# Two-layer decoder on one core: twelve conv pairs of the state-space stage beside the first mixture stage instead of eight

## The reference, cut to what matters

```python
x = x + attention(layernorm(x), Wq, bq, ...)            # A: 16 heads, causal
x = x + token_experts(layernorm(x), tokens, ctx)        # B: 4 experts, the context rows are the weights
x = x + mixture(layernorm(x), gate, w1, w2, shared)     # C: 8 experts, top 2, and one shared expert
x = x + state_space(layernorm(x), in_proj, conv, ...)   # D: the stage that the change is about
x = x + attention(layernorm(x), ctx, ctx)               # E: keys and values are the context rows
x = x + mixture(layernorm(x), ...)                      # F

def state_space(u):                                     # D
    xBC, z, A_log = split(u @ in_proj.T, [1536, 512, 64])
    xBC = silu(causal_conv(xBC, 4 taps, per channel) + bias)
    X, B, C = split(xBC, [512, 512, 512])               # 64 heads x 8;  8 groups x 64;  8 groups x 64
    dt = softplus(A_log)
    y = chunked_scan(X, -dt, B, C, chunk=128) + D * X / dt
    return (y * silu(z + z_bias)) @ out_proj.T
```

## Time and profile before

| | |
|---|---|
| median of 3 runs | 832.39 us |
| profiled execution | 829.35 us, its span 827.5 us |
| mean granted TensorE clock | 0.901 |
| stage C, conv pairs beside it | about 315 to 370 us |
| stage D | about 370 to 590 us |
| DVE busy, span | 543.0 us, 66% |
| PE busy, span | 666.7 us, 81% |

### The profile page before, as it was taken

The page is one execution under the profiler, slowest core; times in us unless marked ns, Lnnn a source line. Parts: engine busy times, 40 slices in busy tenths (PEclk is TensorE's granted clock), DMA queues, the critical chain, the costliest instruction groups (busy, mean ns, idle before and its releaser), DMA issues. The chain is left out here.

```text
span 827.5 us, 16974 instructions
## 1 busy us (share of the span) xinstructions
PE 666.7 (81%) x6016; PEld 496.4 (60%) x6016; DVE 543.0 (66%) x1250; ACT 406.8 (49%) x892; POOL 171.5 (21%) x193
## 2 busy tenths in 40 slices
PE   3688887887878889676698798977678887789996
PEld 2345544464667788563466565654456664778996
DVE  5776755366675356683977998867577847864455
ACT  1235444204254345864577567563246646654553
POOL 5100101121400342007032101131411103103213
PEclk9789999999998899988798799897979986899998
DMA  9800000070212351005000000000033101014433
GB/s 298 288 2 2 2 2 2 1 284 1 71 41 75 124 158 40 19 22 135 3 6 7 1 8 6 7 7 2 1 122 119 67 3 41 31 52 154 142 108 116
DMA packets 39070, 53.10 MB, mean 64 GB/s; under 512 B 9874, under 2 KB 33170, under 8 KB 38558
## 3 DMA queue, kind: packets, MB, share of 16 engines
q1 hardware_dynamic: 35918, 43.62, 16.0%
q0 software_dynamic: 3072, 8.39, 3.3%
HBM read 37.97 MB, written 17.04 MB: 66 GB/s over the span
## 5 line engine op out<-in xcount | busy, mean ns | idle before, releaser
L1169 ACT ACTIVATE s_mega<-bank 128x512 f32<-128x512 f32 x96 | 56.0, 598 | 63.8 <-PE bank L1579 41.7
L2157 DVE TENSOR_TENSOR s_mega<-bank,s_mega 128x176 f32<-128x176 f32 x84 | 28.4, 338 | 77.8 <-ACT s_mega L1224 77.6
L2016 DVE TENSOR_REDUCE s_mega<-bank 128x2 f32<-128x512 f32 (+1 forms) x96 | 62.8, 683 | 15.0 <-PE bank L1543 8.7
L2219 DVE SCALAR_TENSOR_TENSOR s_mega<-s_mega,s_convw 128x256 f32<-128x256 f32 x144 | 68.2, 514 | 1.8 <-ACT s_mega L1286 0.8
L2284 DVE TENSOR_TENSOR s_mega<-s_mega 128x512 f32<-128x512 f32 x64 | 47.1, 742 | 13.1 <-ACT s_mega L1379 10.3
L1224 ACT ACTIVATE s_mega<-bank 128x176 f32<-128x176 f32 x84 | 26.8, 319 | 56.0 <-PE bank L1737 55.7
L1022 POOL DMA_INDIRECT xd<-s_xn,s_pos x32 | 33.5, 1047 | 94.7 <-issue 94.7
L1747 PE MATMUL bank<-s_ident,s_mega 128*88 128x128 f32 x168 | 34.9, 292 | 21.5 <-DVE s_mega L2157 21.5
L1387 ACT ACTIVATE s_mega<-bank 128x512 f32<-128x512 f32 x64 | 37.9, 602 | 24.9 <-PE bank L1847 24.6
L1032 POOL DMA_INDIRECT s_mega<-yd,s_pos x32 | 31.7, 989 | 74.9 <-DMA yd<-s_mega 59.7
L968 POOL TENSOR_TENSOR s_rstd<-s_ve,s_mhalf 128x2 f32<-128x2 f32 x24 | 16.8, 698 | 141.5 <-DVE s_ve L1930 129.9
(11 more groups left out here) (278 smaller groups left out, 1948.8 us busy)
## 6 DMA issues: line engine op xcount, KB each, us to landing
s_mega<-xd SPq DMA_DIRECT2D x60, 128.0 KB, 2.1
yd<-s_mega SPq DMA_DIRECT2D x60, 128.0 KB, 1.7
s_wrawF<-in_wF SPq DMA_DIRECT2D x10, 608.0 KB, 5.3
s_wrawC<-in_wC SPq DMA_DIRECT2D x9, 608.0 KB, 10.2
xd<-in_zeros SPq DMA_DIRECT2D x2, 1920.0 KB, 18.2
s_mega<-in_win SPq DMA_DIRECT2D x1, 2112.0 KB, 9.8
s_mega<-in_hots SPq DMA_DIRECT2D x2, 704.0 KB
s_x<-in_x SPq DMA_DIRECT2D x4, 256.0 KB, 4.6
```

Source lines behind the costliest of these rows:

```text
L1169: a.activation(PT[:, p % NPT, :], AR[n % 3][:, :], ACT.Exp).then_inc(a_read, 1)
L2016: v.tensor_reduce(nM[:, q, h0:h0 + heads], W[n % 3][:, :].rearrange("p (h k) -> p h k", h=heads), AX.X, ALU.max, negate=True).then_inc(w_r ...
L2219: ins = v.scalar_tensor_tensor(o, raw[:, m % NRAW, h, KS - 1 - k:KS - 1 - k + L], convw[:, ct, KS - 1 - k:KS - k], o, ALU.mult, ALU.add)
```

## The change

1. `BESIDE_C` and `FIRST_PAIRS` go from 8 to 12: all pairs of batches 0 and 1 run beside stage C, in block steps 22 + 6, 7, 7, 8, 8, 9, 10, 10, 11, 12, 12, 13. The other twelve run in stage D, from slot 24 on, three every 16 slots, instead of sixteen from slot 0 on.
2. Tiles 4 to 11 of batch 1 are kept in `ctxn`'s memory (`xs_of`), and the context rows are loaded there in stage D, when the state matmuls of unit 3 are done, on the SP queue. Who reads them waits for a semaphore of its own.
3. Beside stage C, ev of pair m waits for the taps of pair m-2, where it waited for that pair's silu.

```diff
-BESIDE_C = 8
-FIRST_PAIRS = 8
+BESIDE_C = 12
+FIRST_PAIRS = 12
+PAIR_STEPS_IN_C = (6, 7, 7, 8, 8, 9, 10, 10, 11, 12, 12, 13)
+PAIRS_FROM = NHG + NHG // 2
...
                 for m in range(beside_c):
-                    j = q + 6 + m if m < 6 else q + 9 + m - 6
-                    j = (q + 6, q + 7, q + 8, q + 9, q + 10, q + 11, q + 12, q + 13)[m]
+                    j = q + PAIR_STEPS_IN_C[m]
                     at_step(j, *((kind, nxt, divmod(m, PAIRS)) for kind in ("din", "din2", "ev")))
                     at_step(j + 1, *(("tap", nxt, (*divmod(m, PAIRS), k)) for k in range(1, KS)))
                     at_step(j + 2, *((kind, nxt, divmod(m, PAIRS)) for kind in ("th", "silu")))
...
-                            put(NHG * u + p, "tap" if kind in (1, 2, 3) else kind, (*pair, kind) if kind in (1, 2, 3) else pair)
+                            put(PAIRS_FROM + NHG * u + p, "tap" if kind in (1, 2, 3) else kind, (*pair, kind) if kind in (1, 2, 3) else pair)
...
+        xs_lent = ctxn[:, :, :].rearrange("p n d -> p (n d)").rearrange("p (i t) -> p i t", t=L)
+
+        def xs_of(b, first_, last_):
+
+            return xs_lent[:, first_ - 4:last_ - 4, :] if b == 1 and first_ >= 4 else xs[:, b % 2, first_:last_, :]
...
-            sp.dma_start(ctxn[:, :, :], ctx_v).then_inc(ctx_in, 16)
...
+                elif kind == "state" and i == 2 * NT - 1:
+
+                    sp.wait_ge(v_full, at["V"]["state", s, i, 1] + 1)
+                    sp.dma_start(ctxn[:, :, :], ctx_v).then_inc(ctxn_in, 16)
...
-                    if m >= NRAW:
+                    if m >= NRAW and m < beside_c:
+                        act.wait_ge(conv_done, (KS - 1) * (m - NRAW + 1))
+                    elif m >= NRAW:
                         act.wait_ge(xs_ready, m - NRAW + 1)
```

More of the change, by code:

```diff
@@ L682, in decoder @@
         x_in = [sem(f"x_in{b}") for b in range(B)]
-        const_in, attn_in, out_in, ctx_in, tok_in, gate_in, mix_in = sems(
-            "const_in attn_in out_in ctx_in tok_in gate_in mix_in")
+        const_in, attn_in, out_in, ctx_in, ctxn_in, tok_in, gate_in, mix_in = sems(
+            "const_in attn_in out_in ctx_in ctxn_in tok_in gate_in mix_in")
         hot_in = [sem(f"hot_in{i}") for i in range(2)]
@@ L942, in _ @@
                         load_rows(1)
-            for landed, loads in (*((x_in[b], 1) for b in range(B)), (tok_in, 1), (const_in, 4), (attn_in, 3), (out_in, 2), (ctx_in, 2), (gate_in, 4), (mix_in, 6)):
+            for landed, loads in (*((x_in[b], 1) for b in range(B)), (tok_in, 1), (const_in, 4), (attn_in, 3), (out_in, 2), (ctx_in, 1), (ctxn_in, 1), (gate_in, 4), (mix_in, 6)):
                 sp.wait_ge(landed, 16 * loads)
@@ L988, in _ @@
                         else:
-                            pool.wait_ge(ctx_in, 32)
+                            pool.wait_ge(ctxn_in, 16)
                         if k >= 3:
@@ L1180, in _ @@
                     k = attn_index(s, i)
-                    act.wait_ge(ctx_in, 32)
+                    act.wait_ge(ctxn_in, 16)
                     act.wait_ge(xn_ready, ln_index(s, i) + 1)
@@ L1283, in _ @@
                         ct = 2 * j + h
-                        a.activation(xs[:, b % 2, ct, :], pair[:, h, :], ACT.Identity,
+                        a.activation(xs_of(b, ct, ct + 1)[:, 0, :], pair[:, h, :], ACT.Identity,
                                      bias=convw[:, ct, KS:KS + 1], scale=convw[:, ct, KS - 1:KS])
@@ L1292, in _ @@
                     if m < beside_c:
-                        half = xs[:, b % 2, 2 * j:2 * j + 2, :]
+                        half = xs_of(b, 2 * j, 2 * j + 2)
                         a.activation(half, half, ACT.Silu, scale=2.0).then_inc(xs_ready, 1)
                         continue
-                    a.activation(raw[:, m % NRAW, :, KS - 1:], xs[:, b % 2, 2 * j:2 * j + 2, :], ACT.Tanh
+                    a.activation(raw[:, m % NRAW, :, KS - 1:], xs_of(b, 2 * j, 2 * j + 2), ACT.Tanh
                                  ).then_inc(tanh_ready, 1)
@@ L1492, in _ @@
                     if s == "B":
-                        pe.wait_ge(ctx_in, 32)
+                        pe.wait_ge(ctx_in, 16)
                     if s in "CF":
@@ L1828, in _ @@
                     banks = [v_bank("cb", s, i, par) for par in range(2)]
-                    B_, C_ = (xs[:, b % 2, 4 * n:4 * n + 4, c * P:(c + 1) * P] for n in (1, 2))
+                    B_, C_ = (xs_of(b, 4 * n, 4 * n + 4)[:, :, c * P:(c + 1) * P] for n in (1, 2))
                     for g2_ in range(NG // 2):
@@ L1879, in _ @@
                                 mm(banks[par][HS * h:HS * (h + 1), g2_ * NS:(g2_ + 1) * NS],
-                                   xs[rows, b % 2, 8 + g2_, P + HS * h:P + HS * (h + 1)], (stt, st2)[h][rows, g2_, :],
+                                   xs_of(b, 8, 12)[rows, g2_, P + HS * h:P + HS * (h + 1)], (stt, st2)[h][rows, g2_, :],
                                    start=(g2_ == 0), stop=(h == 0), skip_group_check=True)
@@ L1962, in _ @@
                         if k % B == 0:
-                            dve.wait_ge(ctx_in, 32)
+                            dve.wait_ge(ctxn_in, 16)
                         if i == 0 and begun_in_d:
```

10 lines of the change are left out of this document (5 added, 5 removed).

## The result

The changed kernel takes 859.23 us (median of 4 runs, 853.57 to 862.9) against 833.02 for the kernel before beside it (832.22 to 833.85): a ratio of 1.0326 [1.028, 1.0372]. The forecast was 843.0 with 831 to 852 around it. The direction is right, the size is not, and the time lies outside the range.

What follows compares the result with a forecast made beforehand. A chain PE - ACT - DVE through one PSUM bank (T), all three in order, was taken to bound stage C's tail. 832.39 plus 21.0 (tail) minus 10.4 (stage D) gave 843.0 us, with 8 in 10 expected in 831 to 852.

Steps and rivals of the forecast that it cites:

- the term of +21.0: Tail of stage C: four more pairs, with two projections through bank T in four steps, add 21.0 us; bounds 2.1 to 23.5.
- The walk's sum: Tail of stage C, steps 29 to 36: delays added step by step through the queues, 20.9 us, called 21.
- Units 0 and 1, -13.7: Stage D: 3 pairs fewer in unit 0 give 8.0 us, 2.33 fewer in unit 1 give 5.7.
- units 2 to 4 taken as unchanged: Stage D: each unit priced by its pair count; these hold 3 pairs before and after, so no change in time.
- the D term: Stage D: unit 0 gives 8.0 us, unit 1 5.7, unit 5 takes 3.3; net 10.4 shorter, bounds 2.4 to 12.9.
- The last conv pair: Stage D: still ends at slot 90 of 94 when its reader comes; nothing new is late there.
- the state reads of batch 2: Stage D: state of unit 1 is read at slot 20, ev waits for it come at slot 24 or later, already met.
- the context load: Stage D, unit 3: rows land by 489.2 us at the latest, unit 4 needs its own at 497.28; costs nothing.
- Waits take it: Tail of stage C: DVE's 14.1 us of waits absorb the added taps, tail only +2.1, total 824.1 us; chance 0.17.
- One turn a pair: Tail of stage C: four turns of 3.5 us at full clock, no ev held by taps, +14.0, total 836.0; chance 0.17.
- the load is late: Stage D, unit 4: waits for its rows behind the context load, +3.6 us on top, total 846.6; chance 0.03.
- Unit 0 not shorter: Stage D: unit 0 is held by gathers and norms, stage gives only 2.4 us, total 851.0; chance 0.09.

Runs made afterwards that it cites:

- e10: Changed kernel with the later 12 pairs in their old slots and a second PSUM bank for pairs 2, 4, 7 and 10: 831.36 us, 0.9995.
- e1: Changed kernel with the later 12 pairs back in their old stage D slots, all twelve early pairs still beside stage C: 838.61 us, 1.0092.
- e2: Kernel before with only the shift: pairs 12 to 23 from slot 24 on, pairs 8 to 11 in their old slots: 852.79 us, 1.0265.
- e5: Changed kernel with stage E's norm moved from the end of an even unit to slot 3 of the odd one: 851.65 us, 1.0249.
- e13: Changed kernel with the first pair of each three 5 slots earlier (4 in some marks), the other two as changed: 847.45 us, 1.0184.
- e12: e5 with each pair's marks put behind the unit's own marks of the same slot: 849.0 us, 1.0216.
- e3: Kernel before with only batch 1's tiles kept in the context buffer and the context rows loaded at unit 3, its own pairs: 831.92 us, 1.0014.
- e4: e1 with the twelve projections one a step, in steps 28 to 39, so no step has two: 836.22 us, 1.0062.
- e9: e1 with the second projection of a step moved to the middle of the next step: 840.06 us, 1.0117.
- e8: Kernel before with pairs 8 and 9 moved into the steps before slot 2, pairs 10 and 11 into unit 0: 829.78 us, 0.9991.

## Why the prediction was wrong

**What bounds the tail, and the term of +21.0: right.** The walk's sum from step to step was 3.6, 8.5, 8.9, 14.3, 14.7, 18.3, 20.4, 20.9. Measured, by the multiplies and less the 2.75 that were there before: 3.4, 8.6, 9.8, 14.4, 15.9, 18.8, 21.3, 21.0. The projection behind the long gap took 3.75 instead of the 3.3 assumed, the two steps with a single projection some 0.8 and 1.1 us more than their 0.4; steps 34 and 36 took 0.7 less each. The wait after step 34 was 2.9, not 4 or more. That T is the reason was an argument then; e10 shows it for half of it. The other half equals what DVE has to work more (10.5 us); the walk came to it through turns of T and the raw buffers, which no run tried one by one. One reading was wrong and entered only the first rival's sum: the 4.14 us at 326.94 stand ahead of the first table load (327.71), not behind one. ScalarE waited there for the projection that follows the step-size chain's own turn of T (its copy at 322.72, the projection at 323.19).

**Units 0 and 1, -13.7: right in sum, where the pairs stand well.** With the old slots (e1), where unit 1 keeps two pairs and unit 5 its one, the same price per pair gives -8.0 - 2.5 = -10.5; measured -13.3, 1.3 of it in unit 2. In the changed kernel unit 0 gave 9.1, and unit 1, from which 2.33 pairs went, 2.8 instead of 5.7.

**The step that failed: units 2 to 4 taken as unchanged.** The prediction counted pairs by unit ("with the shift by one and a half units they hold 0, 0.67, 3, 3, 3, 2.33") and priced each unit by its count, so that units 2, 3 and 4 cost nothing. They cost 3.4 + 3.6 + 8.9 = 15.9, and 16.1 is what the D term is wrong by (+5.7 for -10.4; what units 0, 1 and 5 missed by cancels to 0.2). The median lies 16.2 above the forecast. The price per pair was taken from units in which every pair stands at its old slot, and holds for those alone. e2 (22 us from the slots with nothing else changed) and e1 (19.5 back) show it from both sides. For the tail the prediction walked each step through the queues that it passes; for the later pairs' own new places it did not: not through bank R, which they share with xt, nor through POOL's order of products and rstd. Walking one unit at its new slots as the tail was walked would have met xt behind two turns of R.

**What is settled of the shift's cost, and what stays open.** Of 19.5 us, the norm behind POOL's products is 6.4 (e5), and the first pair of each three 11.8 (e13); the two overlap, since e13 takes 3.1 us of the same wait away. The order within a slot is none of it that shows (e12). What is left is some 4 to 8 us: 7.7 after e13, and 4.4 if the other 3.3 of e5 come on top, which no run tried. Whether that is taps of two pairs meeting across the unit's end or the pairs' share in R, and which of the two the 11.8 of the first pair are, no run tells apart.

**The last conv pair, the state reads of batch 2, and the context load: right**, e3 costing 0.14% with no change in its interval, and no wait for any of them in the trace; the load landed 5.9 us after its issue.

**The rivals.** "Waits take it" did not come: DVE's idle time in the ten steps rose from 17.9 to 28.4 us. "One turn a pair" had 14.0 for the tail's 21.0, and "the load is late" did not occur. "Unit 0 not shorter" gave the nearest time, 851.0, for a reason that did not occur either. None named the later units: the range was made of doubts about terms in the sum, and the mistake was a term left out.

**Was there anything in the change?** With the old slots and a second bank (e10) the stage D gain, 13.7, pays the tail's 11.0 and a little more behind it; in the timed runs the two kernels are equal. Of the 11.0, 10.5 are added work of DVE; to gain more, the taps would have to go into the 18 us in which DVE still stands idle in these steps, and no version does that. None of the versions beats the kernel before.

## What to carry to other kernels

When a hand-written order is shifted, the number of items in each stretch is not its price: walk one period at the new places, queue by queue and bank by bank, and look for in-order engines on which two chains change places. Look also at what stays when the waits are gone. Two turns of one PSUM bank in a step made DVE stand idle 10.5 us longer here, and a second bank (e10) or one turn a step (e4) took most or all of that away; moving the turn within the next step (e9) only moved the wait. What stayed every time was the moved pairs' own work on DVE. And if a range is only as wide as the doubts about the terms that one wrote down, ask for a bound for those called unchanged.

## What was not expected of the hardware

After the same gap the clock falls in one execution and not in the other. At step 33 PE waits 2.18 us for the same copy in the kernel before and in e8, which does the same work up to there; the projection behind it, first before, then in e8 (timeline of PE):

```profile
347.36 1.10 PE L1772 MATMUL bank<-s_xnT,s_mega 128*128 128x256 f32 x4 [0.59 <-issue]
348.30 1.03 PE L1779 MATMUL bank<-s_xnT,s_mega 128*128 128x256 f32 x4
```

```profile
350.96 2.04 PE L1781 MATMUL bank<-s_xnT,s_mega 128*128 128x256 f32 x4 [0.51 <-issue]
352.80 1.91 PE L1788 MATMUL bank<-s_xnT,s_mega 128*128 128x256 f32 x4
```

1.97 us at a granted clock of 1.00 against 3.75 at 0.50. With the 40 matmuls of stage A (3.60 or 4.48 us), some 2 to 5 us of the span, by estimate from these rows and from the 4.6 us by which step 28 differs between the profiles, hang on such places, whatever the change: a difference of that size between two single profiles says nothing until it is seen where it arises.
